# Attention on one Trainium2 core: two heads side by side in TensorE's row halves, fp32 probabilities and values

## What is computed

```python
# 1. per image: attention over pixels with 32 channels, no scale, no mask, one head
q, k, v = wq @ xf, wk @ xf, wv @ xf                 # (b, 32, 1024)
x = xf + wo @ (softmax_j(k_i . q_j) v_j)            # softmax over j of a 1024 x 1024 matrix
t = x as tokens                                      # (4, 1024, 64)
# 2. causal attention: LayerNorm over 64 channels, 8 heads of 64, scale 1/8
q, k, v = (ln(t) @ Wq, ln(t) @ Wk, ln(t) @ Wv)       # (4, 8, 1024, 64)
t = t + softmax(causal(q k^T / 8)) v @ Wo
# 3. ln(t) @ W^T, batch norm over all tokens, gamma, beta, then a recurrence over the 1024 tokens
y[s] = sigmoid(wx[s] + y[s-1] @ V^T);  out = t + y
```

## Time and profile before

| what | us |
|---|---|
| runs | 649.3, 653.6, 654.26; median 653.6 |
| the profiled execution, its own time | 655.42 |
| the span in its profile, first to last instruction | 653.6 |
| TensorE matmuls busy | 535.2 (82%) |
| VectorE busy | 497.6 (76%) |
| ScalarE busy | 468.7 (72%) |
| GpSimd busy | 442.0 (68%) |

### The profile page before, as it was taken

The page is one execution under the profiler, slowest core; times in us unless marked ns, Lnnn a source line. Parts: engine busy times, 40 slices in busy tenths (PEclk is TensorE's granted clock), DMA queues, the critical chain, the costliest instruction groups (busy, mean ns, idle before and its releaser), DMA issues.

```text
span 653.6 us, 17645 instructions
## 1 busy us (share of the span) xinstructions
PE 535.2 (82%) x6985; PEld 348.9 (53%) x6985; DVE 497.6 (76%) x1060; ACT 468.7 (72%) x891; POOL 442.0 (68%) x401
## 2 busy tenths in 40 slices
PE   3777769799779999878989977878999988984694
PEld 0234347466546666546666644555666655663241
DVE  4667877688888778888778888886777888845568
ACT  2167648998748888757888865567888867892673
POOL 2455647978848878757878874476888767893003
PEclk9978769999979999989999998799999989996798
DMA  8000000000000000000000000000000000000001
GB/s 225 33 2 2 1 1 3 2 2 2 3 2 2 2 3 2 2 1 3 2 2 3 2 2 2 3 1 1 2 3 2 2 2 3 3 3 2 0 0 64
DMA packets 2784, 6.46 MB, mean 10 GB/s; under 512 B 1008, under 2 KB 1296, under 8 KB 2576
## 3 DMA queue, kind: packets, MB, share of 16 engines
q1 hardware_dynamic: 2336, 4.30, 2.4%
q10 hardware_dynamic: 368, 1.05, 0.5%
HBM read 4.22 MB, written 1.05 MB: 8 GB/s over the span
## 4 chain that ended last, share of the span: by engine, by line
PE 48%; DVE 31%; ACT 8%; POOL 6%; issue 5%; DMA 1%; DVEq 0%; SPq 0%; ACTq 0%; POOLq 0%
PE bank L355 7%; DVE attn_partial_max L667 7%; POOL probs_low L637 5%; PE bank L381 5%; PE bank L382 5%; PE bank L318 4%; PE bank L408 4%; DVE queries_low L660 4%; PE bank L412 4%; PE bank L410 4%; ACT queries_high L540 4%; PE bank L319 3%; PE bank L514 3%; DVE probs_low L637 2%; DVE conv_partial_max L656 2%
## 5 line engine op out<-in xcount | busy, mean ns | idle before, releaser
L637 POOL TENSOR_TENSOR probs_low<-probs,probs_high 128x512 f16<-128x512 f32 x312 | 374.7, 1223 | 135.2 <-ACT probs_high L553 134.9
L552 ACT ACTIVATE probs<-bank 128x512 f32<-128x512 f32 x352 | 219.3, 623 | 26.3 <-PE bank L384 19.3
L553 ACT ACTIVATE probs_high<-bank 128x512 f16<-128x512 f32 x352 | 220.6, 627 | 0.0
L667 DVE TENSOR_REDUCE attn_partial_max<-bank 128x1 f32<-128x512 f32 (+2 forms) x288 | 195.1, 686 | 24.8 <-PE bank L355 16.9
L408 PE MATMUL bank<-values_high,probs_high 128*128 128x65 f16 x1408 | 169.8, 198 | 6.0 <-POOL probs_low L637 2.5
L410 PE MATMUL bank<-values_low,probs_high 128*128 128x64 f16 x1408 | 169.8, 196 | 0.0
L412 PE MATMUL bank<-values_high,probs_low 128*128 128x65 f16 x1408 | 169.5, 196 | 0.0
L408 PEld LDWEIGHTS bank<-values_high,probs_high 128*128 128x128 f16 x1408 | 135.8, 100 | 31.2 <-issue 7.3
L410 PEld LDWEIGHTS bank<-values_low,probs_high 128*128 128x128 f16 x1408 | 133.9, 101 | 21.6 <-issue 4.2
L355 PE MATMUL bank<-attn_keys,queries_high 128*128 128x512 f16 (+3 forms) x384 | 117.1, 332 | 34.2 <-DVE attn_partial_max L667 22.2
L412 PEld LDWEIGHTS bank<-values_high,probs_low 128*128 128x128 f16 x1408 | 134.0, 100 | 0.0
(11 more groups left out here) (152 smaller groups left out, 737.3 us busy)
## 6 DMA issues: line engine op xcount, KB each, us to landing
x_channels<-in_x_cm SPq DMA_DIRECT2D x7, 256.0 KB, 9.0
tokens<-in_x_tm SPq DMA_DIRECT2D x1, 1024.0 KB, 12.0
out<-ln_channels SPq DMA_DIRECT2D x4, 256.0 KB, 2.0
queries_high<-minus_max_rows SPq DMA_DIRECT2D x36, 2.0 KB
attn_weights<-in_attn_w ACTq DMA_DIRECT2D x1, 512.0 KB, 8.6
x_channels<-in_x_cm ACTq DMA_DIRECT2D x1, 256.0 KB, 3.7
constants<-in_const ACTq DMA_DIRECT2D x1, 256.0 KB, 5.9
conv_weights<-in_conv_w SPq DMA_DIRECT2D x1, 128.0 KB, 2.4
```

The source lines that it names most:

```text
L552: nc.scalar.activation(e32[:, i % E_RING, :], o[:], ACT.Exp, scale=scale)
L553: nc.scalar.activation(p_hi[:, i % P_RING, :], o[:], ACT.Exp, scale=scale).then_inc(s_probs, 1)
L637: eng.tensor_tensor(out=p_lo[:, i % P_RING, :], in0=e32[:, i % E_RING, :], in1=p_hi[:, i % P_RING, :], op=ALU.subtract).then_inc(done, 1)
L667: nc.vector.reduce_max(dst, src, AX).then_inc(s_prep_used, 1)
```

## The change

Two heads of the same image become one unit of 18 items ("a pair"), head `r` in rows 64`r` to 64`r`+63 of queries and keys; conv units stay as they are. Items of a pair of heads are issued two at a time, in even slots.

- **Scores.** High and low parts of the keys are now two tensors, each with the same values in both row halves. One item takes three products with 64 rows (high x high, high x low, low x high), and the two heads' matmuls alternate, each into its own bank. The masks are issued first, for both heads, with all 128 rows.
- **Row maxima** likewise: one product of 64 rows per head, alternating.
- **Queries** of two heads come from one pair of products (`queries` in `AUXES`, bank `AUX`), 2 x 512 columns. They leave the ring of two banks.
- **Probabilities** are one exponential to fp32. The values table is fp32 too, with the two heads side by side. Per block there is one fp32 matmul call instead of three in fp16. `rest_item` is gone, so are the low parts of probabilities and values.
- **Norms.** GpSimd subtracts the mean and multiplies by the reciprocal deviation (`pool_ln1`, `pool_ln3`). VectorE keeps the statistics. The keys are transposed in fp32 (8 per image), and two DMAs per image fill `attn_keys_split`.
- **Order.** `LAG` is 4. In a slot TensorE does values, `AUX` steps, then preparation and scores. VectorE scales first; ScalarE does `AUX` steps first. The ring of probabilities has 10 places.

```diff
-ST_RING, MX_RING, P_RING, E_RING, Q_RING = 3, 2, 8, 6, 3
-LAG, REST_LAG = 5, 3
+ST_RING, MX_RING, E_RING, Q_RING = 3, 2, 10, 3
+LAG = 4
+        def pe_max_masks(m):
+            _, v, k = PREPS[m]
+            nc.tensor.wait_ge(s_prep_used, m + 2 - MX_RING)
+            for r in range(2):
...
+                        nc.tensor.matmul(MX[(m + r) % MX_RING][:, end - P:end], identbf[:], masks[:, 1, :],
+                                         start=not opened, stop=False, skip_group_check=True)
+        def pe_maxes(m):
...
+            for t, j0, tiles, at in runs:
+                for r in range(2):
+                    last[r] = nc.tensor.matmul(MX[(m + r) % MX_RING][:, at * P:(at + tiles) * P],
+                                               q[rows(r), t * P:(t + 1) * P],
+                                               xs_hi[rows(r), b * N + j0 * P:b * N + (j0 + tiles) * P],
+                                               start=not masked, stop=True, skip_group_check=True)
+        def pe_score_masks(i):
+            nc.tensor.wait_ge(s_probs, i + 2 - ST_RING)
...
+        def pe_scores(i):
...
+            for n, (keys, queries) in enumerate(((xs_hi, qh), (xs_hi, ql), (xs_lo, qh))):
+                for j, t0, tiles, at in runs_of(i):
+                    for r in range(2):
+                        last[r] = nc.tensor.matmul(ST[(i + r) % ST_RING][:, at * P:(at + tiles) * P],
+                                                   keys[rows(r), b * N + j * P:b * N + (j + 1) * P],
+                                                   queries[rows(r), t0 * P:(t0 + tiles) * P],
+                                                   start=n == 0 and not masked, stop=n == 2,
+                                                   skip_group_check=True)
         def pe_values(i):
...
-                    nc.tensor.matmul(dst, hi[:, cols], vh[:, j, :], start=opens, stop=False,
-                                     skip_group_check=True)
-                    nc.tensor.matmul(dst[:, 0:C], hi[:, cols], vl[:, j, :], start=False, stop=False,
-                                     skip_group_check=True)
-                    ins = nc.tensor.matmul(dst, lo[:, cols], vh[:, j, :], start=False, stop=True,
-                                           skip_group_check=True)
+                    probs = e32[:, item % E_RING, (at + k) * P:(at + k + 1) * P]
+                    ins = nc.tensor.matmul(OT[half % 2][:, t * PO:t * PO + PO], probs, v32[v % 2][:, j, r, :],
+                                           start=opens, stop=True, skip_group_check=True)
+                for i in TURNS_AT.get(g, ()):
+                    pe_values(i)
                 for m in auxes_at(g):
                     pe_aux(m)
+                for m in singles[:1]:
+                    pe_conv_prep(m)
+                if len(items) == 1:
+                    pe_conv_scores(g)
...
+                for m in pairs:
+                    pe_max_masks(m)
+                if len(items) == 2:
+                    pe_score_masks(g)
+                for m in pairs:
+                    pe_maxes(m)
+                if len(items) == 2:
+                    pe_scores(g)
         def act_item(i):
...
-            nc.scalar.activation(e32[:, i % E_RING, :], o[:], ACT.Exp, scale=scale)
-            nc.scalar.activation(p_hi[:, i % P_RING, :], o[:], ACT.Exp, scale=scale).then_inc(s_probs, 1)
+            nc.scalar.activation(e32[:, i % E_RING, :], ST[i % ST_RING][:], ACT.Exp,
+                                 scale=1.0 if unit_of(i) < B else SCALE).then_inc(s_probs, 1)
-        def rest_item(eng, i, done):
-            eng.wait_ge(s_probs, i + 1)
-            eng.tensor_tensor(out=p_lo[:, i % P_RING, :], in0=e32[:, i % E_RING, :], in1=p_hi[:, i % P_RING, :],
-                              op=ALU.subtract).then_inc(done, 1)
+        def pool_ln1(b):
...
+            pool_link(nc.gpsimd.tensor_tensor(out=xd[:], in0=tok3[:, :, b * C:(b + 1) * C],
+                                              in1=mv1[:, :, 0:1].to_broadcast([P, NT, C]), op=ALU.subtract))
+            for r in range(2):
+                ins = nc.gpsimd.tensor_tensor(out=xh[:, :, r, :], in0=xd[:],
+                                              in1=rstd1[:].unsqueeze(2).to_broadcast([P, NT, C]), op=ALU.mult)
```

More of the change, by code:

```diff
@@ L46 @@
 ]
+SPLIT_ITEM = 2
 ATTN_ITEM_OF_HALF = (2, 8)
@@ new lines, in pe_maxes @@
+        def pe_maxes(m):
+            _, v, k = PREPS[m]
+            b, q = batch_of(v), q_hi[v % Q_RING]
+            if k == 0:
+                nc.tensor.wait_ge(s_aux_used, AUX_OF["queries", 2 * v + 1] + 1)
+            runs = ATTN_MAXES[k // 2][0]
+            masked = any(j0 + tiles - 1 == t for t, j0, tiles, _ in runs)
+            last = [None, None]
+            for t, j0, tiles, at in runs:
[5 more added lines that the diff above has]
+            for r in range(2):
+                last[r].then_inc(s_prep, 1)
@@ L679, in dve_aux, with dve_max_rows @@
+        def dve_max_rows(m):
+            k = AUXES[m][3]
+            tiles = NT if k < B else 2 * NT
+            nc.vector.wait_ge(s_aux, m + 1)
+            nc.vector.tensor_scalar(mrow[k % 2][0:tiles, :], AUX[0:tiles, 0:P], -1.0, None,
+                                    ALU.mult).then_inc(s_aux_used, 1)
         def dve_aux(m):
             _, _, what, k = AUXES[m]
-            if what == "max_transpose":
-                nc.vector.wait_ge(s_aux, m + 1)
-                nc.vector.tensor_scalar(mrow[k % 2][:], AUX[0:NT, 0:P], -1.0, None, ALU.mult).then_inc(s_aux_used, 1)
-            elif what == "conv_matrix":
+            if what in ("conv_matrix", "matrix", "queries", "keys"):
@@ L965, in _ @@
             for g in range(0, LAST_SLOT):
-                if g < ITEMS and not rest_on_dve(g):
-                    rest_item(nc.gpsimd, g, s_rest_pool)
-                for v, c in HALVES_AT.get(g, ()):
-                    pool_add(v, c)
+                for half in HALVES_AT.get(g, ()):
+                    pool_add(half)
+                for b in range(B):
+                    if g == LN1_APPLY_SLOT[b]:
+                        pool_ln1(b)
+                if g == LN3_PAIR_SLOT + 8:
+                    pool.wait_ge(s_rstd3, 1)
+                    pool.wait_ge(s_added, (B + 2 * H) * NC)
+                if g == LN3_THIRD_SLOT + 8:
+                    pool.wait_ge(s_rstd3, 2)
+                    pool.wait_ge(s_added, (B + 3 * H) * NC)
+                for k in range(NC):
+                    if g == LN3_PAIR_SLOT + 8 + 4 * k:
+                        pool_ln3(k, 0, 2, s_l3)
+                    if g == LN3_THIRD_SLOT + 8 + 4 * k:
+                        pool_ln3(k, 2, 3, s_l3t)
             ya, yb = y32[(FULL_SWEEPS - 1) % 2], y32[FULL_SWEEPS % 2]
@@ L1012, with maxrows, values_ready @@
 AUX_OF = {(what, k): m for m, (_, _, what, k) in enumerate(AUXES)}
-CASTS_BY = [sum(k < (4 if v < B else 2) for _, v, k in PREPS[:m + 1]) for m in range(len(PREPS))]
-AUX_CASTS_BY = [sum(what in ("conv_matrix", "values", "matrix") for _, _, what, _ in AUXES[:m + 1])
+CASTS_BY = [sum(v < B and k < 4 for _, v, k in PREPS[:m + 1]) for m in range(len(PREPS))]
+AUX_CASTS_BY = [sum(what in ("conv_matrix", "queries", "matrix", "keys") for _, _, what, _ in AUXES[:m + 1])
                 for m in range(len(AUXES))]
-FIRST_BLOCK = {("conv", 0): (0, 0), ("conv", 1): (NT, 0), ("attn", 0): (0, 0), ("attn", 1): (2, 2)}
-HALVES_AT = {}
-for _v in range(UNITS):
-    for _c in range(NC):
-        HALVES_AT.setdefault(item_of_half(_v, _c) + LAG + 1, []).append((_v, _c))
+TURNS_AT, HALVES_AT = {}, {}
+for _i in range(ITEMS):
+    TURNS_AT.setdefault(turn_slot(_i), []).append(_i)
+for _h, (_, _, _, _i) in enumerate(CLOSED_BY):
+    HALVES_AT.setdefault(turn_slot(_i), []).append(_h)
+def maxrows(v):
+    return 16 * (v + 1) if v < B else 16 * B + 32 * (v - B + 1)
+def values_ready(v):
+    return (AUX_OF["conv_values", v] if v < B else AUX_OF["values", 2 * v + 1]) + 1
 def kernel(x, L0_conv_wq, L0_conv_wk, L0_conv_wv, L0_conv_wo, L1_attn_Wq, L1_attn_Wk, L1_attn_Wv, L1_attn_Wo,
```

523 lines of the change are left out of this document (287 added, 236 removed).

## The result

The kernel with the change takes 685.7 us (median of 4 runs, 683.8 to 688.8), the kernel before 653.1 beside it: a ratio of 1.052, 95% interval 1.046 to 1.057. The forecast was 671 in a range of 636 to 730. The direction and the range held; the loss is 33 us where some 18 were forecast. Executions that were disturbed, at a lower clock and longer (two of four with the conv preparation apart, one of four with the conv products in `AUX`, two of ten of the last fp16 version), are left out of every ratio.

What follows compares the result with a forecast made beforehand. No engine was taken as full: TensorE and VectorE wait for each other over a ring of two banks. 655.4 + 26 (attention) - 6 (conv) - 2 (tail) = 673 us, 671 as a median, range 636 to 730.

Steps and rivals of the forecast that it cites:

- attention, +26: Attention items: 444 us of TensorE, 29 of crossings and 6 of stalls make 479 us, against 452.8 before.
- Values at 2 x 0.11 us a block: Attention values on TensorE: two fp32 matmuls a block, 0.22 us against 0.09; 15.8 us per pair against 6.5.
- Crossings at 0.10: TensorE's changes between 128-row and 64-row matmuls, two a turn: 0.10 us each, 29 us over 144 turns.
- VectorE's slack: VectorE in attention: 2.1 us of work in a turn of 3.3 us, so it has room.
- The first rival: Attention on TensorE: crossings are hidden and row halves overlap fully; 625 us, chance 0.20 for anything below 647.
- the second: Scores and maxima on TensorE: row halves don't overlap, 117 us more; 788 us, chance 0.12.
- the third: VectorE becomes late in the ring of two banks, a turn losing 0.3 us; 714 us, chance 0.10.
- The fourth: TensorE's granted clock falls to 0.90 instead of 0.97 in attention; 720 us, chance 0.08.
- all such stalls: Attention turns: 6 us for late reductions, scalings, norm steps, score banks and the DMA of the maxima.
- Conv items: Conv stretch: 95 us of TensorE plus 5 us for a stall at image 0's norm, 100 us, -6 us.
- my 95 us for TensorE: Conv stretch: TensorE's work, with values 53, scores 14, maxima 10 and smaller terms, 95 us.
- Tail: From last score to last reciprocal, 6.3 us before: scores 0.7, two turns of values 3.6, 0.1, so -2 us.

Runs made afterwards that it cites:

- the conv preparation apart: Changed kernel with images 2 and 3 prepared 16 slots ahead, as image 1 is, instead of 24: 682.4 and 690.0 us.
- the conv products in `AUX`: Changed kernel with the eight products for keys and queries of images 2 and 3 moved from the ring of two banks to `AUX`: 679.1 us, ratio 1.039.
- the last fp16 version: Changed kernel without fp32 values (three fp16 products, two exponentials), VectorE's subtractions first in its slot, on items 3, 8, 13: 649.6 us, ratio 0.993.
- the heads are held apart: Changed kernel with head 0's maxima and scores written before head 1's, and TensorE waiting for head 0's last matmul before head 1: 844.1 us.
- the first fp16 version: Changed kernel without fp32 values (three fp16 products, two exponentials), VectorE's share of subtractions behind its turn's reductions: 701.9 us, ratio 1.079.
- single fp16 products: Changed kernel with probabilities and values in fp16 alone, low parts left out: 538.6 us; with the conv products in `AUX` too, 537.0 us, ratio 0.821.

## Why the prediction was right or wrong

**Right: attention, +26.** Forecast 479 us, measured 478.5. Its main terms hold one by one. Values at 2 x 0.11 us a block: 16 in 1.83 us. Full overlap of row halves: 0.22 us per couple, and of the +153 us when the heads are held apart, 93 are three score products per turn that no longer overlap. Crossings at 0.10: 0.09 to 0.11 in two timelines, and +14.9 us for 144 more. On VectorE's slack: TensorE's matmuls wait 2.5 us in the whole stretch. The first rival needed crossings of 0.04, the second a lost overlap, the third waits for VectorE; none is there. The fourth had the clock fall; it is 1.00 in this stretch. The step from the earlier trace rows to the crossings, one row read in both directions, carried 29 us and was right; by the Trainium skill ("TensorEngine Tiling (Array Packing)", Key Properties) none of them would be free, and none was in these rows.

That the sum met the measurement to 0.5 us is partly luck. Of the 6 us for "all such stalls" only 2.5 show as waits, and the 0.01 us for each of 48 couples (8 us in all) is not there: a set of two heads starts 0.22 us after the last whether a product is one matmul or two. Against that, fp32 matmuls start 0.112 us apart rather than 0.11, some 5 us in 2304 of them; where the rest lies was not sought.

**Wrong: "Conv items", "I put 5 us: 100, -6 us".** Measured 112.1, +6.4. I looked for one stall, the norm of image 0. All norms on VectorE cost 5.8 us more, but the stall that counts is another: each product, cast and subtraction holds one of the two banks while the other is needed for maxima. The prediction noted that the queries of the heads leave that ring and said nothing of the conv products that stay in it. The same chain stood in the kernel before, and its trace had it to read. Two such products in TensorE's timeline there:

```profile
45.12 0.39 PE L318 MATMUL bank<-x_split,conv_weights_high 128*128 128x512 f16 x1 [0.21 <-DVE conv_partial_max L656]
48.75 0.39 PE L318 MATMUL bank<-x_split,conv_weights_high 128*128 128x512 f16 x1 [1.06 <-DVE conv_partial_max L656]
```

They lie 3.63 us apart, in one slot of a stretch that averages 105.7 / 64 = 1.65; what it cost in all was not measured there. Moving the chain out gave back 6.3 of the 12.1 us. The other 5.8 are not settled. TensorE's matmuls are busy for 101 of the 105.8 us now, so they are likely in my 95 us for TensorE, and not in waits. The ordinary slot agrees (0.84 for values and 0.21 each for maxima and scores), so the surplus should lie in the steps that come once, or in the first pair's preparation, which I priced by estimate; that is argued, not shown.

**Wrong: "Tail", -2.** From the last score to the last reciprocal it went from 6.3 us to 4.4, as forecast:

```profile
L810 DVE RECIPROCAL reciprocal_denominators<-bank x72: 165/183/185, 49.7 to 624.1; 128x4 f32<-128x4 f32 x72
```

What follows took 61.2 us instead of 59.3, and the granted clock of the tail was 0.77 against 0.82; in the profiled runs where it was 0.82 the tail took 63.6, 64.1 and 64.4. Whether the clock is the cause was not tried.

**The sum.** 12.1 from conv, 2.0 from the tail and less than 1 from the rest make the 14.5 us between 673 and the profiled execution's 687.5.

**A judgement that was missing.** The prediction priced removed work on ScalarE and GpSimd at nothing, as the chain hardly held them. Put back, it cost up to 21 us over two stretches, and the first fp16 version showed how 44 subtractions, on VectorE there, become a bound once their place in an order is wrong.

## What to carry to other kernels

When precision is bought with more passes, compare them by start-to-start times of the cheapest form: here an fp32 call (two matmuls, two loads, 0.22 us) replaced three fp16 products (0.09), and relieving three engines that weren't the bound could not pay for 149 us on the one that became it. Two heads of 64 rows side by side do run at full overlap; count 0.10 us for each change between halves and whole rows, and group the work so that there are two per turn. And list, for every ring of banks, each step that holds a bank through a cast and a subtraction: such a step beside ordinary ones made a slot of 2.9 us out of 1.5, and moving eight of them to a bank that was idle there gave back 6.3 us.

## What the runs showed of the hardware that was not expected

- Matmuls of the other row half started ahead of earlier instructions of the program. With head 0's six written first, head 1's first one started at 300.61 us, 0.01 us after the first matmul of head 0's second product and ahead of three more that the program has before it. So the overlap doesn't hang on interleaving by hand. That was worth 9 us (694.7 against 685.7), by the two turns above in those where a product is two matmuls.
- Neither the fp32 values (weight loads busy 334 us) nor the crossings cost clock in attention: the granted clock, 0.97 before, is 1.00 there with two crossings a turn and with four. In conv it rose from 0.85 to 1.00, in the same trace in which TensorE's waits shrank. In conv with single fp16 products, where TensorE waits again, it was 0.89 and 0.84, and in three of the fp32 runs 0.97 to 0.99.
- An fp32 call is two matmuls of 0.11 us up to 128 columns, but 0.43 each at 512, twice the 0.216 of fp16. So at 512 columns a call costs as much as four fp16 matmuls. With 64 and with 65 columns it still takes 0.22 us, as with 128, so the columns don't set it; that its two weight loads do (192 ns long each, against 100 in fp16) is my reading. The Trainium skill ("FP8 and Floating Point Precision", TensorE Precision Notes) speaks of four passes for true fp32; the 512-column rows agree.
